# Rounding the weighted expert values on GpSimd instead of ScalarE in a two-layer transformer kernel

## The reference

```python
logits = x @ router_w.T + expert_bias[None, :]
probs = jax.nn.sigmoid(logits)
top_w, top_idx = jax.lax.top_k(probs, TOP_K)                    # TOP_K = 8
top_w = top_w / (jnp.sum(top_w, axis=-1, keepdims=True) + 1e-09)
top_w = top_w * ROUTED_SCALE
combine = jnp.zeros((T, NUM_EXPERTS), dtype=x.dtype)            # NUM_EXPERTS = 160
combine = combine.at[jnp.arange(T)[:, None], top_idx].set(top_w)
h1 = jax.nn.silu(jnp.einsum('th,eih->eti', x, w_gate))          # INTER = 64, HIDDEN = 128
h1w = h1 * combine.T[:, :, None]
routed = jnp.einsum('eti,ehi->th', h1w, w_down)
shared = jax.nn.silu(x @ w_gate_shared.T) @ w_down_shared.T
return (routed + shared).reshape(B, S, H)
```

## Time and profile before

| | us |
|---|---|
| median of 3 runs | 961.28 |
| lowest, highest | 960.23, 965.87 |
| span of the profiled execution | 961.3 |

### The profile page before, as it was taken

The page is one execution under the profiler, slowest core; times in us unless marked ns, Lnnn a source line. Parts: engine busy times, 40 slices in busy tenths (PEclk is TensorE's granted clock), DMA queues, the critical chain, the costliest instruction groups (busy, mean ns, idle before and its releaser), DMA issues.

```text
span 961.3 us, 18422 instructions
## 1 busy us (share of the span) xinstructions
PE 898.8 (93%) x5540; PEld 553.0 (58%) x5540; DVE 673.8 (70%) x1358; ACT 739.6 (77%) x1265; POOL 41.6 (4%) x42
## 2 busy tenths in 40 slices
PE   3779999999999999998799999999999999999997
PEld 2522222245222222877477777777777777777775
DVE  8743642225576200598399999999999999999997
ACT  2769989965988889555488888787888877788886
POOL 4700000000000000040000000000000000000000
PEclk9969999999999999999899999999999999999999
DMA  4000000000000000000677778777778877777873
GB/s 112 1 23 7 7 12 0 0 1 23 2 12 10 3 0 0 2 12 28 168 183 197 201 201 198 196 197 194 196 199 198 196 194 190 203 188 197 197 197 100
DMA packets 68310, 101.94 MB, mean 106 GB/s; under 512 B 29783, under 2 KB 46455, under 8 KB 68279
## 3 DMA queue, kind: packets, MB, share of 16 engines
q1 hardware_dynamic: 68278, 101.54, 42.0%
HBM read 97.04 MB, written 2.36 MB: 103 GB/s over the span
## 4 chain that ended last, share of the span: by engine, by line
PE 71%; DMA 9%; DVE 8%; SPq 3%; ACT 3%; issue 3%; DVEq 1%; POOL 0%; POOLq 0%; ACTq 0%
PE PS L1075 15%; PE PS L1058 14%; DMA wg_raw<-in_L_ffn_w_gate_dram 9%; PE PS L1366 6%; PE PS L1368 6%; PE PS L1367 6%; PE PS L1373 5%; PE PS L1375 5%; PE PS L1374 5%; SPq L231 3%; PE PS L1153 2%; DVE HM L963 2%; PE PS L1345 1%; ACT SI L586 1%; PE PS L1084 1%
## 5 line engine op out<-in xcount | busy, mean ns | idle before, releaser
L441 ACT ACTIVATE E<-PS 128x1024 f32<-128x1024 f32 x256 | 260.6, 1025 | 32.4 <-PE PS L1058 14.3
L586 ACT ACTIVATE SI<-PS 128x512 f32<-128x512 f32 x320 | 191.9, 600 | 85.4 <-PE PS L1368 84.3
L963 DVE TENSOR_TENSOR HM<-SI,CWB 128x512 f32<-128x512 f32 x320 | 221.5, 692 | 37.4 <-ACT SI L586 14.7
L968 DVE TENSOR_TENSOR HLo<-HM,HH 128x512 fp32r<-128x512 f32 x320 | 218.9, 684 | 0.1
L380 ACT ACTIVATE HH<-HM 128x512 fp32r<-128x512 f32 x320 | 199.2, 623 | 4.1 <-DVE HM L963 4.0
L1058 PE MATMUL PS<-QT,KM 128*128 x512 | 156.1, 388 | 11.2 <-DMA KM<-KT 4.9
L1075 PE MATMUL PS<-E,VS 128*32 128x256 f32 x2048 | 160.4, 390 | 0.0
L768 DVE COPY OS<-PS 128x512 f32<-128x512 f32 x16 | 11.1, 692 | 179.8 <-PE PS L1075 179.8
L1366 PE MATMUL PS<-XH,wgH 128*128 128x512 f32 x320 | 134.2, 419 | 0.0
L1373 PE MATMUL PS<-HH,wdH 128*128 128x512 f32 x320 | 128.1, 400 | 0.9 <-DVE HLo L968 0.9
L1375 PE MATMUL PS<-HH,wdL 128*128 128x512 f32 x320 | 126.8, 396 | 0.0
(11 more groups left out here) (215 smaller groups left out, 860.6 us busy)
## 6 DMA issues: line engine op xcount, KB each, us to landing
CWB<-combine_weights SPq DMA_DIRECT2D x320, 256.0 KB, 3.9
wg_raw<-in_L_ffn_w_gate_dram SPq DMA_DIRECT2D x80, 64.0 KB, 3.4
wd_raw<-in_L_ffn_w_down_dram SPq DMA_DIRECT2D x80, 64.0 KB, 3.8
KM<-KT SPq DMA_DIRECT2D x32, 64.0 KB, 2.0
X<-in_L_attn_x_dram SPq DMA_DIRECT2D x4, 256.0 KB, 3.9
combine_weights<-CWT SPq DMA_DIRECT2D x2, 512.0 KB, 2.9
out_dram<-X SPq DMA_DIRECT2D x4, 256.0 KB, 2.9
combine_weights<-CWT SPq DMA_DIRECT2D x2, 128.0 KB, 3.0
```

What stands on the lines that cost most here:

```text
L441: nc.scalar.activation(E[:, u % NE_SLOTS, :], PS[:, 2 * (u % 2):2 * (u % 2) + 2, :], ACT.Exp, scale=SCALE0).then_inc(S["exp_act"], 1)
L586: nc.scalar.activation(SI[:, slot % 2, :], bank(4 + slot % 2), ACT.Silu).then_inc(S["s_act"], 1)
L963: TT(HM[:, slot % 4, :], SI[:, slot % 2, :], CWB[:, q, half, CH * c:CH * c + CH], ALU.mult)\
L968: TT(HLo[:, slot % 4, :], HM[:, slot % 4, :], HH[:, slot % 4, :].bitcast(F32), ALU.subtract)\
```

## The change

`high` moves from ACT's instruction stream to GpSimd's: 320 `tensor_copy` instructions, each after a wait on the constant `count + 1` of `m_dve`, written out without a loop after the last add on `X`. The semaphore that it raises is renamed from `hi_act` to `hi_pool`, and DVE's `low` waits for that one. ACT's `silu` gets the wait on `m_dve` that `high` held ahead of it until now (`SI` has two buffers, so `silu(n)` needs `weigh(n-2)` done); its value is the same as before. No other instruction changes.

```diff
+            def high(slot, count):
+                pool.wait_ge(S["m_dve"], count + 1)
+                nc.gpsimd.tensor_copy(HH[:, slot % 4, :], HM[:, slot % 4, :]).then_inc(S["hi_pool"], 1)
+
+            for n in range(STEPS * (NP // 2)):
+                high(n % STEPS, n)
...
-            def silu(slot, count):
+            def silu(slot, count, free):
                 act.wait_ge(S["g_pe"], count + 1)
+                if free is not None:
+                    act.wait_ge(S["m_dve"], free)
                 nc.scalar.activation(SI[:, slot % 2, :], bank(4 + slot % 2), ACT.Silu).then_inc(S["s_act"], 1)
-
-            def high(slot, count):
-                act.wait_ge(S["m_dve"], count + 1)
-                copy(HH[:, slot % 4, :], HM[:, slot % 4, :]).then_inc(S["hi_act"], 1)
...
-            silu(0, 0)
-            for s in range(1, AHEAD - 1):
-                silu(s, s)
-                high(s - 1, s - 1)
+            for s in range(AHEAD - 1):
+                silu(s, s, s - 1 if s >= 2 else None)
...
-                        silu(s + AHEAD - 1, i * STEPS + (s + AHEAD - 1))
-                    if not (last and s + AHEAD - 2 >= STEPS):
-                        high(s + AHEAD - 2, i * STEPS + (s + AHEAD - 2))
+                        silu(s + AHEAD - 1, i * STEPS + (s + AHEAD - 1), i * STEPS + (s + AHEAD - 2))
...
             def low(slot, count):
-                dve.wait_ge(S["hi_act"], count + 1)
+                dve.wait_ge(S["hi_pool"], count + 1)
                 TT(HLo[:, slot % 4, :], HM[:, slot % 4, :], HH[:, slot % 4, :].bitcast(F32), ALU.subtract)\
```

More of the change, by code:

```diff
@@ L193, in two_block_layer_kernel @@
             "sh_pe sh_act hmask_pool res_pool cws0 cws1 cwl00 cwl01 cwl10 cwl11 wgl0 wgl1 wdl0 wdl1 wg_pe wgh_act wgl_dve "
-            "g_pe d_pe s_act m_dve hi_act lo_dve mt_act fo_pe fo_dve stored"
+            "g_pe d_pe s_act m_dve hi_pool lo_dve mt_act fo_pe fo_dve stored"
         ).split()
```

## The result

| | median us | lowest, highest | runs |
|---|---|---|---|
| before | 960.89 | 960.23, 965.87 | 4 |
| after | 1000.48 | 998.41, 1001.68 | 4 |

The account below looks back on a forecast made before the run. PE was taken to bound the loop at 1.50 us a step. Copy, weigh and low excluding each other would make it 2.0 us: 0.50 us over 320 steps, 160 us on 961.3, 1121, stated as 1125; range 1035 to 1250.

Parts of the forecast that it names:

- The mechanism: Expert loop: GpSimd's copy and DVE's weigh and low, with two SBUF operands each, exclude each other; the second stands still.
- The sum: Expert loop: copy, weigh and low add up to a step of 2.0 us against 1.50, 160 us over 320 steps.
- The order: Expert step: copy between low and weigh, 1.86 us, or DVE first with both, 2.2 us; 2.0 taken as about the middle.
- The copy's length: GpSimd's 128x512 copy in each step: 0.70 us, from 0.10 fixed and 1.18 ns a column; bounds 0.53 and 1.21.
- The start: Blocked instructions in the loop: DVE's weigh counted as 0.69 - 0.14 = 0.55 us, GpSimd's copy at its full 0.70.
- The overlap: DVE in the loop: blocked weigh counted at 0.55 us, then low at its spacing of 0.61 us.
- No blocking: Expert loop: copies run beside DVE, PE stays the bound, 961 us within 1%; chance 0.09.
- Cheap blocking: Expert loop: copy 0.53 us, turn between low and weigh, step 1.69 us, 1022 us in all; chance 0.12.
- Expensive rounding: GpSimd's copy in the loop takes 1.21 us, step 2.7 us, 1345 us in all; chance of over 1250: 0.09.
- Loss of clock: PE in the loop drops to its low clock, six matmuls 2.5 us, 1313 us in all; chance 0.04.
- The `w_low` pair: DVE's two short w_low instructions, one operand in PSUM, run beside a copy at no cost when it goes before weigh.
- Handovers: Turn changes between GpSimd and DVE: about 115 ns each, two a step would add 74 us, to about 1196.

Follow-up runs that it names:

- The earlier load: Each gate-weight load issued two steps earlier, directly after the down-weight load: 947.49 us in the kernel before, 1000.31 us in the changed kernel.
- the copy twice: Changed kernel with a second GpSimd copy of the same HM, into a tile nobody reads, ahead of each rounding copy: 1155.85 us.
- The half copy: Kernel before plus one GpSimd copy of 256 columns a step between tiles nobody else uses, nothing waiting for it: 967.18 us, ratio 1.0040.
- the foreign copy: Kernel before, ScalarE still rounding, plus one GpSimd copy of 128x512 a step between tiles nobody else uses, nothing waiting for it: 1002.67 us.

## Why the prediction was wrong in size

**What bounds the kernel.** Right: PE before, and ScalarE's 199 us worth nothing. The earlier load gained 16 us where PE's waits counted.

**The mechanism.** Right, and it was shown by runs of its own: the loss exists with a copy that nobody waits for, vanishes when GpSimd only writes, and vanishes when one operand of the blocked DVE instruction is in PSUM. The rows of contention in other stages of the kernel before carried over to these instructions.

**The sum.** This is the step that failed: a step of the loop was put at 2.0 us and is 1.61. Over 320 steps that is the whole miss, and it has four terms.
- *The order.* 2.0 was the middle of two orders, 1.86 and 2.2. Only the first occurs: the copy is issued 0.14 us after `low` starts and 0.47 us before `weigh`, and it gets its turn first. This choice cost 0.14 us a step. With the copy twice, turns again go by the order of the requests. That order could have been had from the earlier trace rows: `low` starts 0.08 us before `weigh` ends, so a copy that waits for that `weigh` asks while `low` runs and well ahead of the next `weigh`. Averaging over orders was a way of not working this out.
- *The copy's length.* 0.70 us by extrapolation from a copy of 256 columns; undisturbed it takes 0.61. Cost 0.09. The half copy shows which part was off. Its 0.26 us after `low` and the 0.14 us of start make 0.40 us for 256 contiguous columns, as an estimate, the same as the 0.402 us of the earlier trace rows, where they are cut into runs of eight. The rate between 256 and 512 columns is 0.82 ns, the memset's (0.83). That leaves a fixed part of some 0.19 us; the sum had taken the memset's 0.10 for it and put the rest on the columns. The 769 ns that the prediction took from the Trainium skill (GPSIMD Engine Reference, "Elementwise — side-by-side cycle accounting") as a price for the copy is not borne out: the page has that figure for an unrolled elementwise loop, and this copy takes 611 ns.
- *The start.* The blocked instruction goes through its start while it waits. I allowed for this on DVE (0.14 us) and not on GpSimd, where only 0.54 of 0.61 us shows between the issue of `weigh` (701.34) and the copy's end (701.88). Cost 0.07. The prediction had read "its whole length" off, 1.00 us after the release; in the loop the copy ends 0.47 us after `low` does.
- *The overlap.* The next DVE instruction starts 0.08 us before the one ahead ends. It was in the spacing of 0.61 and then lost where a duration (0.55) and a spacing were added. Cost 0.08.

So 1.86 - 0.09 - 0.07 - 0.08 = 1.62 for the first order, in a mechanism that was otherwise right. Each term is small, but only what exceeds PE's step counts, 0.12 us here. The miss of 0.39 us a step is a fifth of the step and three times the loss. That is how a range that looked wide, 1035 to 1250, lay wholly above the result: its lower end was a step of 1.73, and even the first order with the copy's measured 0.61 us makes 1.77 as long as the last two terms are missing.

**The rivals.** No blocking: refuted, by the foreign copy. Cheap blocking: nearest in time (1022), partly by luck. Its copy of 0.53 us was 0.08 too short, and it left out the last two terms (0.15), so its step of 1.69 stands 0.07 above the measured one. Nor does the copy block for only part of its length: `weigh` gets through 0.55 us after the copy's end. Expensive rounding: no, with the conversion to fp32r the copy takes 0.61 us, less than the 0.70 extrapolated from the plain one. Loss of clock: no, 1.00 from 500 to 900.

**The `w_low` pair** was costed at nothing and is nothing: it runs while the copy does, and the `weigh` behind it takes 0.70 us. The weights' step thus repays 0.40 us of blocking with its own 0.40 us of work, and all four steps come out at 1.62 (703.97 to 705.59 here). From the kernel after:

```profile
703.97 0.68 DVE L969 TENSOR_TENSOR HLo<-HM,HH 128x512 fp32r<-128x512 f32 x1
704.57 0.28 DVE L954 TENSOR_TENSOR wgL<-PS,wgH 128x128 fp32r<-128x128 f32 x1
704.97 0.70 DVE L964 TENSOR_TENSOR HM<-SI,CWB 128x512 f32<-128x512 f32 x1
705.59 0.68 DVE L969 TENSOR_TENSOR HLo<-HM,HH 128x512 fp32r<-128x512 f32 x1
```

**Handovers.** The Trainium skill (SBUF — State Buffer, "A bandwidth-pool intuition that's wrong") has its figure of about 115 ns from a DMA whose descriptors GpSimd writes, held up behind DVE. The 0.23 us a step that it would add here, as an estimate, is not there: `weigh` ends 0.55 us after the copy, which is its length of 0.69 less its start of 0.14. The 4 us by which the forecast was rounded up for handovers had nothing behind them either.

## What to carry to other kernels

- Before work goes to an idle GpSimd, look at what VectorE does beside it: a tensor_tensor with both inputs in SBUF is blocked by a GpSimd instruction that reads SBUF. A write on GpSimd, or one PSUM operand on VectorE, avoids it. Look in the trace for such a pair that already overlaps in another stage; here the blocking seen there carried over.
- Where engines exclude each other, write the order of requests down from the timeline and add what each turn shows; then subtract what the bounding engine left free. A loss is a difference of two near numbers, so an error of 5% in the sum is not one of 5% in the loss.
- A wait that grows after a change need not be its cause. Here PE's wait for the DMA doubled, and taking it away changed nothing.

## What was not expected of the hardware

- A blocked instruction carries the wait in its own duration, on both engines (1.01 for 0.61 us on GpSimd, 1.09 for 0.69 us on DVE), with no idle time ahead of it. The prediction had read this off; what it means for the reader of a page is that idle times and releasers show nothing of such a loss, and the mean of the line does.
- Turns went in the order of the requests in every case shown here, and a handover cost nothing that shows (0.54 or 0.55 us for a blocked `weigh` of 0.69, 0.47 or 0.48 for a blocked copy of 0.61).
- By the estimate above, a GpSimd copy costs a column no more than a memset does (0.82 against 0.83 ns); what it has more is the fixed part, some 0.19 us against 0.10.
- GpSimd blocked by DVE costs nothing where its result has slack; with Silu in PSUM the median copy took 1.01 us in place of 0.61, at 964.79 us.
